# Fp32 softmax weights as stationary operand of the value products in the first two blocks of a token-tower kernel

## What is computed

```
h = rms_norm(proj(rms_norm(emb[x]) * w))
q, k, v = (layernorm(h) @ w for w in (wq, wk, wv))
att = softmax(causal(q @ k.T / sqrt(16)));  y = att @ v
h = h + y @ wo
z = layernorm(h)
h = h + (silu(z @ w_gate.T) * (z @ w_up.T)) @ w_down.T
```

## Time and profile before

| what | us |
|---|---|
| median of 3 runs | 752.84 (749.26, 752.84, 752.88) |
| the profiled execution, its own time | 748.56 |
| its span, first to last instruction | 746.8 |
| PE busy | 686.7 |
| DVE busy | 444.3 |
| ACT busy | 358.4 |
| POOL busy | 355.2 |

### The profile page before, as it was taken

How to read it: one execution, slowest core, us unless ns; L and a number is a source line. 1 busy time by engine, 2 the same in 40 slices (tenths; PEclk the granted TensorE clock), 3 DMA queues, 4 the chain that set the end, 5 groups by cost and what they waited for, 6 DMA issues and landing times.

```text
span 746.8 us, 16350 instructions
## 1 busy us (share of the span) xinstructions
PE 686.7 (92%) x6314; PEld 511.6 (68%) x6314; DVE 444.3 (59%) x1072; ACT 358.4 (48%) x725; POOL 355.2 (48%) x449
## 2 busy tenths in 40 slices
PE   7636878868899999999999999999999999999998
PEld 4434647755489847985699659964897489857873
DVE  6888989889565546645565546563655465444320
ACT  6955656666256513662266316641565146521320
POOL 7024535787237543664266516653465437530220
PEclk9957899999999999999999999999999999999999
DMA  8959020001100011001200120003000210000000
GB/s 323 415 165 352 18 89 3 1 1 40 50 29 2 3 59 59 2 1 46 73 1 3 39 79 2 2 1 103 16 2 2 66 51 2 2 15 15 1 1 29
DMA packets 10461, 40.39 MB, mean 54 GB/s; under 512 B 1808, under 2 KB 2576, under 8 KB 8592
## 3 DMA queue, kind: packets, MB, share of 16 engines
q1 hardware_dynamic: 6912, 25.44, 8.8%
q0 software_dynamic: 3328, 13.11, 5.6%
q10 hardware_dynamic: 144, 0.79, 0.3%
HBM read 29.89 MB, written 9.44 MB: 53 GB/s over the span
## 4 chain that ended last, share of the span: by engine, by line
PE 73%; DVE 13%; POOL 4%; issue 4%; ACT 3%; DMA 3%; SPq 0%; DVEq 0%; POOLq 0%; ACTq 0%
PE banks L1079 12%; PE banks L1081 12%; PE banks L1080 12%; PE banks L1107 6%; PE banks L1109 6%; PE banks L1108 6%; PE banks L995 3%; PE banks L1036 2%; PE banks L1038 2%; PE banks L1037 2%; PE banks L984 2%; DVE gate_work L779 1%; PE banks L1008 1%; DVE ffn_weights L732 1%; PE banks L1009 1%
## 5 line engine op out<-in xcount | busy, mean ns | idle before, releaser
L1079 PE MATMUL banks<-xnT_and_h,ffn_weights 128*128 128x256 f16 x1024 | 279.6, 273 | 3.3 <-DVE ffn_weights L732 3.3
L1081 PE MATMUL banks<-xnT_and_h,ffn_weights 128*128 128x256 f16 x1024 | 279.8, 273 | 0.0
L1080 PE MATMUL banks<-xnT_and_h,ffn_weights 128*128 128x256 f16 x1024 | 279.6, 273 | 0.0
L360 POOL TENSOR_TENSOR gated_split<-gate_work,gated_split 128x256 f16<-128x256 f32 x128 | 86.5, 676 | 238.2 <-ACT gated_split L495 238.0
L364 POOL TENSOR_TENSOR weights_split<-weights,weights_split 128x512 f16<-128x512 f32 x128 | 153.3, 1199 | 19.5 <-ACT weights_split L501 19.5
L1079 PEld LDWEIGHTS banks<-xnT_and_h,ffn_weights 128*128 128x128 f16 x1024 | 100.2, 98 | 15.2 <-issue 3.7
L485 ACT ACTIVATE gate_work<-banks,scales 128x256 f32<-128x256 f32 x128 | 60.4, 472 | 100.6 <-PE banks L1081 100.6
L1081 PEld LDWEIGHTS banks<-xnT_and_h,ffn_weights 128*128 128x128 f16 x1024 | 100.3, 98 | 11.9
L1080 PEld LDWEIGHTS banks<-xnT_and_h,ffn_weights 128*128 128x128 f16 x1024 | 100.3, 98 | 11.5
L491 ACT ACTIVATE weights<-banks,scales 128x512 f32<-128x512 f32 x128 | 87.1, 681 | 36.5 <-PE banks L995 36.4
L757 DVE COPY q_stack<-banks 128x256 f16<-128x256 f16 x128 | 36.8, 288 | 106.3 <-PE banks L984 106.1
(11 more groups left out here) (228 smaller groups left out, 1065.2 us busy)
## 6 DMA issues: line engine op xcount, KB each, us to landing
ffn_weights<-in_ffn_w SPq DMA_DIRECT2D x12, 1024.0 KB, 14.9
out_rows_dram<-ffn_weights SPq DMA_DIRECT2D x16, 256.0 KB, 2.0
xnT_and_h<-in_wqkv SPq DMA_DIRECT2D x1, 1536.0 KB, 8.4
local_table<-gated_split SPq DMA_DIRECT2D x2, 640.0 KB, 5.9
local_table<-xnT_and_h SPq DMA_DIRECT2D x2, 640.0 KB, 3.6
gated_split<-in_projT SPq DMA_DIRECT2D x4, 256.0 KB, 4.3
ffn_weights<-in_wo SPq DMA_DIRECT2D x1, 1024.0 KB, 10.4
token_table<-weights_split ACTq DMA_DIRECT2D x1, 768.0 KB, 8.7
```

The costliest lines, as they stand in the source:

```text
L360: g.tensor_tensor(gtl[:, j, :], g2[j % 2], gth[:, j, :], ALU.subtract).then_inc(gt_lo, 1)
L1079: t.matmul(o, wh, xTh[m % 2][:, c, :], start=c == 0, stop=False)
L1080: t.matmul(o, wh, xTl[m % 2][:, c, :], start=False, stop=False)
L1081: last = t.matmul(o, wl, xTh[m % 2][:, c, :], start=False, stop=c == DC - 1)
```

## The change

For the first 32 units (`WIDE`, blocks 0 and 1) the weights are not split: the fp32 tile `weights` is the stationary operand of 4 products, each with 17 moving fp32 columns (`v_full_one`, which POOL adds up once from the high and low v). ACT then makes no high part and POOL no low part there. In block 0 DVE divides y straight out of PSUM and there is no ACT copy, with a second PSUM bank for the odd pairs of the first tile; in block 1 ACT still copies and POOL only divides. The q stacks of both blocks move from DVE to ACT. All high halves of the weight chunks are ACT's. Value products come two slots after the score for these units, not three. The slot tables of phase 0 are written anew: the first tile's `yt` is at slot 11 instead of 13, the group maxima at slots 0 to 7 instead of 4 to 11, GRAM at 16 to 20 instead of 6 to 16, the fillers of slots 0 to 19 are gone, and the bound step and its product are at 21 and 22. The first gate and up products stand ahead of the first turn of block 1. The pieces below are, in this order, of the constants and of the programs of POOL, ACT, DVE and PE.

```diff
+VFW = HD + 1
+WIDE = 2 * UPB
...
-FIRST_SLOTS = dict(yt=(13, 20), wo=(15, 21), ln=(16, 21), xhat=(16, 21), xn=(19, 22), fetch=(20, 22), m=(23, 3))
+FIRST_SLOTS = dict(yt=(11, 18), wo=(13, 19), ln=(16, 20), xhat=(17, 20), xn=(19, 21), fetch=(17, 20), m=(21, 3))
...
-LOW_FIRST = {20: (0, 1), 21: (2,), 23: (3,)}
+LOW_FIRST = {18: (0,), 20: (1,), 21: (2,), 23: (3,)}
...
-FILL = {**{s: 2 for s in range(17)}, 17: 4, 18: 4, 19: 4, 20: 4, 21: 6, 22: 6}
+FILL = {20: 6, 21: 6, 22: 4}
...
-GROUP_SLOTS = range(4, 12)
-GRAM = {s: (6 * (s - 6), min(64, 6 * (s - 5))) for s in range(6, 17)}
-DN_BOUND_SLOT, DN_SUM_SLOT, DN_MAX_SLOT, DN_SCALE_SLOT = 19, 21, 23, 3
-GU_SCALE_SLOT = 2
+GROUP_SLOTS = range(0, 8)
+GRAM = {16: (0, 8), 17: (8, 16), 18: (16, 32), 19: (32, 48), 20: (48, 64)}
+DN_BOUND_SLOT, DN_SUM_SLOT, DN_MAX_SLOT, DN_SCALE_SLOT = 21, 22, 23, 3
+GU_SCALE_SLOT = 8
...
+            pool.wait_ge(tab["vl"], 1)
+            g.tensor_tensor(Vf3[:, :, 0:HD], Va3[:, :, 0:HD], Va3[:, :, HD:2 * HD], ALU.add).then_inc(tab["vf"], 1)
...
-                    if att and 1 <= s <= UPB:
+                    if att and 1 <= s <= UPB and n * UPB + s - 1 >= WIDE:
...
+            def stack(V):
+                actq.wait_ge(q_tr, V + 1)
+                if V >= RING:
+                    actq.wait_ge(scores, V - RING + 1)
+                r = V % RING
+                a.activation(Qst[:, r * 256:(r + 1) * 256], b_Q[:, 0:256], ACT.Copy).then_inc(q_st, 1)
...
+                    if n == 1 and s == 0:
+                        split_high(HI_NEXT[0])
+                        stack(UPB)
+                    if att and n <= 1 and s + 1 < UPB:
+                        stack(n * UPB + s + 1)
...
+                    if n == 0 and 3 <= s < UPB + 3 and s % 2 == 1:
+                        k, i = divmod((s - 3) // 2, 4)
+                        pair = 4 * k + i
+                        dve.wait_ge(pv_rdy, 2 * pair + 2)
+                        pv = pv_bank(pair)[:, 0:2 * REP * VFW].rearrange("p (h c) -> p h c", c=VFW)
+                        v.reciprocal(rden[k][:, 8 * i:8 * i + 8], pv[:, :, HD]).then_inc(rd_rdy, 1)
+                        dve.wait_ge(rd_rdy, pair + 1)
+                        yv = y[k][:, i * P:(i + 1) * P].rearrange("p (h d) -> p h d", d=HD)
+                        v.tensor_tensor(yv, pv[:, :, 0:HD], rden[k][:, 8 * i:8 * i + 8].unsqueeze(2).broadcast_to([P, 8, HD]),
+                                        ALU.mult).then_inc(pv_ev, 1)
...
+                if V < WIDE:
+                    pe.wait_ge(w_rdy, V + 1)
+                    if V == 0:
+                        pe.wait_ge(tab["vf"], 1)
+                    for h in range(REP):
+                        o = pv_bank(V // 2)[:, ((V % 2) * REP + h) * VFW:((V % 2) * REP + h + 1) * VFW]
+                        last = t.matmul(o, E[r][:, h * P:(h + 1) * P], Vf3[:, gr, :], start=True, stop=True)
+                    last.then_inc(pv_rdy, 1)
+                    return
...
+                    if ffn and m == 0 and s == 0:
+                        gate_up(0, 0)
+                        turn(UPB)
```

More of the change, by code:

```diff
@@ L97, in lm_block @@
         Va3 = Va[:, :].rearrange("p (g c) -> p g c", g=KV)
+        Vf = sb("v_full_one", KV * VFW, F32)
+        Vf3 = Vf[:, :].rearrange("p (g c) -> p g c", g=KV)
         ident = sb("ident", P, F32)
@@ L107, in lm_block @@
         rden = [sb(f"rden{i}", HEADS, F32) for i in range(TPB)]
[L108 removed]
+        st = sb("ln_stats", 52, F32)
         sc = sb("scales", 64, F32)
@@ L188, in tail, with pv_bank, lag, ev_slot @@
             return f_bank[0] if t == 0 else b_tail
+        def pv_bank(pair):
+            return f_bank[1] if pair < UPB // 2 and pair % 2 == 1 else b_PV
+        def lag(V):
+            return 2 if V < WIDE else 3
+        def ev_slot(pair):
+            return 2 * (pair % (UPB // 2)) + 1 + lag(2 * pair)
         x_in, emb_in, embT_in, nw_in, w_in, wo_in = (sem(n) for n in ("x_in", "emb_in", "embT_in", "nw_in", "wqkv_in", "wo_in"))
@@ L501, in phase @@
                         a.activation(WTh[V % RING], E[V % RING][:, :], ACT.Copy).then_inc(wt_hi, 1)
-                    if att and 4 <= s < UPB + 4 and s % 2 == 0:
-                        i = (s - 4) // 2
+                    for i in range(UPB // 2):
+                        if not (att and n > 0 and s == ev_slot(n * UPB // 2 + i)):
+                            continue
                         k, gp = divmod(i, 4)
@@ L533, in phase @@
                             split_high(HI_FIRST[s])
-                    if n == 1 and s in HI_NEXT:
+                    if n == 1 and s > 0 and s in HI_NEXT:
                         split_high(HI_NEXT[s])
+            stack(0)
             phase(0, True, False, 0)
@@ L864, in _ @@
             place_max(0)
-            stack(0)
             phase(0, True, False, 0)
@@ L1010, in values, with gate_up @@
                 last.then_inc(pv_rdy, 1)
+            def gate_up(m, s):
+                i = m * HC + s
+                if s == 0:
+                    pe.wait_ge(xt_lo, m * TPB + TPB)
+                    if m > 0:
+                        pe.wait_ge(g2_rdy, i)
+                if s == 2 and m == 0:
+                    pe.wait_ge(tab["dn_max"], 1)
+                if s in (1, 2) and m > 0:
+                    pe.wait_ge(fin_rdy, (m - 1) * TPB + s)
+                if s >= 3:
+                    pe.wait_ge(g2_rdy, i - 2)
+                if m == 0:
+                    pe.wait_ge(split_lo, s + 1)
+                for up in range(2):
+                    o = f_bank[s % 3][:, up * BLK:(up + 1) * BLK]
+                    for c in range(DC):
+                        wh, wl = (gu_w(s, up, c, h) for h in (0, 1))
+                        t.matmul(o, wh, xTh[m % 2][:, c, :], start=c == 0, stop=False)
+                        t.matmul(o, wh, xTl[m % 2][:, c, :], start=False, stop=False)
+                        last = t.matmul(o, wl, xTh[m % 2][:, c, :], start=False, stop=c == DC - 1)
+                last.then_inc(gu_rdy, 1)
             def phase(n, att, ffn, m):
@@ L1018, in phase @@
                         turn(n * UPB + s + 1)
-                    if att and 3 <= s < UPB + 3:
-                        values(n * UPB + s - 3)
+                    for u in range(UPB):
+                        if att and s == u + lag(n * UPB + u):
+                            values(n * UPB + u)
                     for k in range(TPB):
```

122 lines of the change are left out of this document (46 added, 76 removed).

## The result

The changed kernel takes **745.36 us** (median of 7 executions, 743.29 to 746.85); the kernel before took 752.88 beside it (7 executions, 748.61 to 754.17). The ratio is 0.9911, with a 95% interval of 0.989 to 0.9932: faster by 0.9%. I had 740, a range of 729 to 750, and a chance of 0.78 for faster.

The account below looks back on a forecast made before the run. PE bounds from block 2 on; gains had to come from phase 0 and phase 1's first 16 slots, where DVE was busy. -3.9 - 7.5 + 0.5 = -10.9 us: 737.7 from the profiled execution, 741.9 from the median; 740 taken, range 729 to 750.

Parts of the forecast that it names:

- the second rival: Phase 0: PE stays at 1.2 GHz, slots of 2.2 us, first gate product at 113, total 747 us; chance 14%.
- Slot 11 is reached between 65 and 80, I take 69.: Phase 0: cheaper slots, costing PE 0.9 to 2.4 us each, bring slot 11 at about 69 us.
- The group table: Phase 0: the group maxima table queues behind four 1 MB pairs, lands at 77.3 and holds ACT before the first `yT`.
- The sum of phase 0: Phase 0, up to the first gate product: 106.0 instead of 109.89 us, -3.9, bounds 103 and 110.
- that `yT` starts before 75: Phase 0: sign against the forecast, the first `yT` on ACT starting before 75 us instead of waiting until about 77.
- the mark on the clock: End of phase 0: sign against the forecast, granted clock at 1.2 GHz when `wo` of tile 1 runs.
- Phase 1: First 16 slots: without POOL's weight subtractions DVE falls to about 48 us, PE becomes the bound, 59.5 instead of 66.98, -7.5.
- the fp32 unit: Phase 1, PE: a unit's 8 fp32 instructions take 0.56 to 0.96 us at full clock, 0.75 taken; 14 units, 10.5 us.
- The rule that I weighed and left: Phase 1, PE: 107 ns per fp32 load makes a unit 0.85 us and the first 16 slots 1.4 us longer.
- The stack on ACT: Phase 1, ACT: one q stack a slot, between 0.28 and 0.68 us, taken as 0.36.
- The bound step: End of phase 0: DVE's maxima, a chunk and the bound take 2.4 us, PE's waiting product and 4 fillers 1.1.
- The last 8 slots: Phase 1, 31.54 us before: two fp32 units replace three fp16 on PE, +1.5 - 0.6, partly inside a wait: +0.5.

Follow-up runs that it names:

- fill_more: The changed kernel with 6 fillers of 512 columns in each of phase 0's slots 0 to 2 and 3 in slots 3 to 15: 741.88 us, ratio 0.9851.
- the upper halves alone: The changed kernel, block 0's value products taking only the upper 16 bits of E and V: 739.17 us; with the group maxima table issued before the pairs, 732.2.
- the doubled kernel: The changed kernel with each fp32 value product of block 1 issued twice: 759.9 us, one execution.

## Why the prediction was right, and where not

**The time.** 740 against 745.36, faster as forecast, inside the range, and partly by luck: the sum was -10.9 us; the profiled executions differ by 2.6, and only the medians by 7.5. The 4.9 us between these two differences are in no row and no term of the prediction. What happened in phase 0 is the second rival, "PE stays at 1.2 GHz in phase 0", to which I had given 14%: slots of 2.2 us (2.27), first gate product at 113 (111.72), 747 us (745.36).

**The step that failed** is this one: "Slot 11 is reached between 65 and 80, I take 69." It came at 77.3. I had taken a value between two clocks, where the change decides which it is: it took out the fillers of slots 0 to 19. Two pairs of kernels that differ in their fillers alone show the cause. The mean clock up to the first gate product is 0.84 with fillers and fp16, 0.68 without the early ones; with fp32 it is 0.67 without them (the changed kernel) and 0.94 with enough of them (fill_more). Without fillers and with the upper halves alone it is 0.69. So the missing fillers cost phase 0 its clock. Whether the kind of product counts beside them is not settled: with fp32 the clock stayed low while PE was busy for 28.00 of 28.00 us, two fillers a slot raised it in three executions of five only, and no run has fp16 products on a full PE without fillers. The fp32 products set what the low clock costs, 0.209 us an instruction, 1.67 a unit. I had 0.22 for it, from the earlier trace rows, so the price was right and the clock wrong.

**The group table.** The sum of phase 0 stood on ACT held until 77.3. In the changed kernel this never showed, since the slots took until then anyway, and my mark against the forecast ("that `yT` starts before 75") was not the way in which it failed. Nor did the mark on the clock show it: when `wo` of tile 1 ran, from 99.04, the clock was back at 2.4 GHz (1.00 from 99.5 to 104); it had been down where I had no mark, in the slots before. Where the slots are short it is there, with its size: 7.54 us, ending at 77.69, and gone when the table is issued first.

**Phase 1.** Right in mechanism as far as shown: POOL's 128x512 subtractions held DVE's chunk step (1504 against 788 ns), and the change turned the stretch over to PE, DVE at 48. That DVE's share is what freed PE, and not ACT's roundings that left with it, is argued. Of my marks, DVE under 50 us, PE over 95% and the fp32 spacing of 0.07 to 0.12 (0.109) came true; of the chunk subtractions the second did (788 ns), the first is over my 1.0 us (1152). Mis-sized was one term, the fp32 unit: I took 0.75 us from rows with 1 and 3 columns; it is 0.87 (0.89 in the doubled kernel), and 15 units fall in the stretch, not 14. 15 x 0.87 - 10.5 = 2.6 us, which is the 2.4 between 59.5 and 61.94. The rule that I weighed and left, 128/1.2 = 107 ns for a load without fast path (the Trainium skill, "TensorE: Matmul & The Clock Gate", sections LDWEIGHTS and Weight-path perf modes), gives 0.85 a unit and was the better price. The measured 0.109 agrees with it at full clock; at the low clock the same instruction takes 0.209, which the page's figure doesn't tell.

**Smaller terms.** The stack on ACT takes 0.381 us, I had 0.36, and its place is worth nothing. The bound step was a wait on the path, 2.27 us; I had 3.5 for it with what stands behind, and moving it gave 3.6. The last 8 slots: +0.5 forecast, +1.0 measured; the fall of the clock alone is 1.3 (30.32 against 29.01 us for the same work), so without it the term is slightly below nothing. The step from the profiled execution to the median, by which I took 740 between 737.7 and 741.9, had the right direction, but no cause behind it; the sum itself, 737.7, stands against 745.95, and phase 0 is 5.7 of these 8.2 us (111.72 against 106.0), the 16 slots 2.4.

## What to carry to other kernels

Before taking a stretch's gain from cheaper work on DVE or POOL, ask which clock PE will have in it: fillers that look like waste may be what keeps the real products at full pace, and their number is to be tried, here with more in the first few slots than in the rest. Look then at the end of the program: of 8.4 us saved ahead of a stretch, 4.2 were left in the time. Price fp32 products of few columns by their loads, 0.11 us an instruction and two instructions a product at full clock, twice that at the low one; they pay where they take work off a chain of other engines that PE waits for (block 1: 6.8 us). And a small table issued behind megabytes on the same queue arrives with them: issue it first.

## What the hardware showed that I had not expected

- In the changed kernel PE was busy for 28.00 of the 28.00 us from 60 to 88 us and stayed at 1.2 GHz. With two fillers a slot it was busy for 18.00 of 18.00 from 62 to 80 (the execution of 755.87 us), over a quarter of it with products of 512 columns, and stayed there too; other executions of that kernel have a mean clock of 0.977 to 0.984 instead of 0.957. The Trainium skill ("TensorE: Matmul & The Clock Gate", Part 1) says that the gate goes by how busy PE has been; by the profile's busy time these traces disagree.
- An instruction of an fp32 product of 17 columns goes with the clock: 0.109 us at 2.4 GHz, 0.209 at 1.2. 120 more of them took 0.112 each.
- A chunk subtraction on DVE takes 1504 ns with POOL's subtractions of the weights beside it and 788 without them, both means over a stretch of over 60 us in which DVE has the same work otherwise.
- The transfer of 128 KB took 11.3 us behind four of 1 MB and 1.7 ahead of them (the kernels with the upper halves alone); in the changed kernel, where it was issued 5 us later (71.37 against 66.26), it took 6.0 and landed at the same time, 77.4 against 77.6.
